# Feature interaction with attention: W's outputs and the pairs in halves, side by side on partitions

## What is computed

```python
e = jnp.stack([tbl_0[ids[:, 0]], ..., tbl_32[ids[:, 32]]], axis=1)       # 512 x 33 x 128
row, col = np.triu_indices(33, k=1)
inner = e[:, row] * e[:, col]                                            # 512 x 528 x 128
fm = relu(einsum('bpd,ad->bpa', inner, attn_W) + attn_b)
scores = einsum('ba,bpa->bp', gnn_feature, fm)
attn = softmax(scores, axis=1)
attn_output = einsum('bp,bpd->bd', attn, inner) * 100.0
h = concatenate([gnn_feature, attn_output, gnn_feature], axis=1)         # 512 x 384
y = relu(relu(h @ W_top1 + b_top1) @ W_top2 + b_top2) @ W_top3
```

## Time and profile before

| | |
|---|---|
| median of 3 runs | 659.28 us (658.95 to 659.39) |
| the profiled execution | 656.88 us, span 655.1 us |
| PE busy | 644.7 us, 98% |
| VectorE busy | 403.9 us, 62% |
| ScalarE busy | 434.0 us, 66% |
| GpSimd busy | 267.6 us, 41% |
| DMA | 17.28 MB, 24 GB/s to and from memory |

### The profile page before, as it was taken

One profiled execution on the slowest core, in us unless ns is written; L12 is line 12 of the kernel. 1 busy time (PEld: TensorE's weight loads), 2 busy tenths in 40 slices (PEclk: granted clock), 3 DMA queues, 4 the chain that ended last, 5 costly groups with the idle time before them and its releaser, 6 DMA issues.

```text
span 655.1 us, 22427 instructions
## 1 busy us (share of the span) xinstructions
PE 644.7 (98%) x9476; PEld 332.8 (51%) x9476; DVE 403.9 (62%) x426; ACT 434.0 (66%) x797; POOL 267.6 (41%) x208
## 2 busy tenths in 40 slices
PE   6999999999999999999999999999999999999998
PEld 2444444444444555444444555554444555545566
DVE  3555656565655667756565577765655567764763
ACT  2676677667777666766777666667677666677651
POOL 6888867585557223144746522234101011100010
PEclk9999999999999999999999999999999999999999
DMA  3311111120091111000092111000026011030020
GB/s 117 86 33 38 41 29 30 25 75 15 18 38 26 30 28 22 19 14 14 14 34 28 29 30 27 15 19 6 1 15 15 7 19 16 7 21 7 16 25 8
DMA packets 51285, 17.28 MB, mean 26 GB/s; under 512 B 47553, under 2 KB 48321, under 8 KB 51202
## 3 DMA queue, kind: packets, MB, share of 16 engines
q1 hardware_dynamic: 44738, 6.03, 11.2%
q0 software_dynamic: 4288, 8.66, 5.4%
q10 hardware_dynamic: 2176, 1.32, 0.7%
HBM read 14.10 MB, written 1.89 MB: 24 GB/s over the span
## 4 chain that ended last, share of the span: by engine, by line
PE 90%; POOL 4%; DMA 3%; issue 1%; DVE 1%; SPq 1%; ACT 0%; DVEq 0%
PE x_ps L465 65%; PE s_ps L477 16%; POOL rows L363 4%; PE m_ps L523 4%; PE m_ps L484 2%; DMA rows<-in_table,idx 1%; PE s_ps L563 1%; PE x_ps L563 1%; DMA band_scratch<-attn 1%; PE x_ps L523 1%; DMA idx_in<-in_ids 0%; DVE inner L749 0%; DMA tail_band<-band_scratch 0%; SPq L270 0%; PE m_ps L552 0%
## 5 line engine op out<-in xcount | busy, mean ns | idle before, releaser
L692 ACT ACTIVATE fm<-x_ps,ab 128x352 f32<-128x352 f32 x768 | 422.6, 554 | 188.4 <-PE x_ps L465 166.5
L465 PE MATMUL x_ps<-inner,attn_w_t 128*32 128x352 f32 x6144 | 478.7, 459 | 0.2 <-DVE inner L749 0.2
L465 PEld LDWEIGHTS x_ps<-inner,attn_w_t 128*32 128x32 f32 x6144 | 202.5, 110 | 225.6 <-issue 135.4
L749 DVE TENSOR_TENSOR inner<-e_t 128x2112 f32<-128x2112 f32 (+1 forms) x128 | 302.3, 2362 | 19.2 <-PE x_ps L465 16.7
L363 POOL DMA_INDIRECT rows<-in_table,idx x128 | 210.3, 1643 | 198.5 <-PE s_ps L477 183.1
L477 PE MATMUL s_ps<-fm,gnn_col 128*32 128x256 f32 (+1 forms) x2048 | 137.7, 386 | 0.0
L765 DVE COPY gnn_col<-gnn_z 128x8 f32<-128x8 f32 (+1 forms) x120 | 23.9, 199 | 183.9 <-PE s_ps L477 183.9
L477 PEld LDWEIGHTS s_ps<-fm,gnn_col 128*32 128x32 f32 x2048 | 68.5, 110 | 62.3 <-issue 19.0
L391 POOL TENSOR_TENSOR band<-band 128x192 f32<-128x192 f32 (+1 forms) x39 | 26.8, 687 | 145.1 <-DMA band<-band_scratch 144.6
L523 PE MATMUL m_ps<-band,rows 128*32 128x132 f32 x912 | 33.6, 275 | 0.0
L523 PEld LDWEIGHTS m_ps<-band,rows 128*32 128x32 f32 x912 | 28.0, 109 | 7.0
(11 more groups left out here) (53 smaller groups left out, 82.1 us busy)
## 6 DMA issues: line engine op xcount, KB each, us to landing
band<-band_scratch SPq DMA_DIRECT2D x144, 18.4 KB, 1.7
rows<-in_table,idx POOLq DMA_INDIRECT x128, 3.1
band_scratch<-zeros SPq DMA_DIRECT2D x1, 784.0 KB, 3.4
w<-in_W_top ACTq DMA_DIRECT2D x3, 256.0 KB, 3.6
band_scratch<-attn SPq DMA_DIRECT2D x12, 64.0 KB
gnn_z<-in_gnn_pairs SPq DMA_DIRECT2D x1, 512.0 KB, 6.0
w<-in_W_top ACTq DMA_DIRECT2D x1, 512.0 KB, 3.9
gnn_t<-in_gnn_cols SPq DMA_DIRECT2D x1, 256.0 KB, 3.9
```

The source lines that it names most:

```text
L465: mm = pe.matmul(strip(x_ps[:, (ROUNDS * slot + r) % 4, 0:ROUND], c), strip_of(attn_w_t, c), round_of(inner, slot, r), start=True, stop=True)
L692: act.activation(round_of(fm, slot, r), x_ps[:, (ROUNDS * slot + r) % 4, 0:ROUND], ACT.Relu, bias=ab[:, 0:1]).then_inc(fm_ready, 1)
L749: dve.tensor_tensor(inner[:, slot, :, :].rearrange("p q (i k) -> p q i k", k=HOPS), flat(e, at, [[P * WIDE, P], [WIDE, QUADS], [1, FIELDS] ...
```

## The change

The 128 outputs of W are cut in two halves of 64, and the 528 pairs of a sample in two halves of 264 (d from 1 to 8, and from 9 to 16). A round of PE is now one sample and one half of W: strips 0 and 1 work on the first half of the pairs, strips 2 and 3 on the second, so that a PSUM bank holds 64 outputs of 264 pairs on partitions 0 to 63 and the same outputs of the other 264 pairs on partitions 64 to 127. There are eight rounds of 264 columns a step.

The relus come out scaled: |g| relu(x + b) = relu(|g| x + |g| b), with `size` = |g| as scale and `shift` = |g| b as bias, both one value per partition. VectorE adds the two halves of W with their signs (`add_halves`, a scalar_tensor_tensor: second half times `turn_sign`, the product of the two signs, plus the first). The scores are then one matmul a sample over 264 columns with weights that are plus or minus one: two columns of a 32-column matrix, one for each half of the pairs. These weights lie in `diag`, which `set_diag` fills for four steps at once.

A sample's scores now take two rows of 264. A row group of 32 holds 16 steps, so a softmax stage is half a tile (`REGION`), in one of two PSUM banks; the last tile has stages of steps 0 to 15, 16 to 27 and 28 to 31. Maximum and sum are exchanged between neighbouring rows with `stream_shuffle`. The band is stored with 8 + 8 DMAs a stage. In the last tile five batches are pooled within the steps, from step 22 on, and 17 groups in the tail. The zeros of the band matrix are cleared by VectorE at the very start and stored then. `zeros`, `tail_band`, `h1` and `h2` share memory with `rows`. All loops over steps are unrolled. The core of the diff, with long stretches left out:

```diff
-            def pair_products(n, slot, first=False):
...
-                for r in range(ROUNDS):
...
-                        mm = pe.matmul(strip(x_ps[:, (ROUNDS * slot + r) % 4, 0:ROUND], c), strip_of(attn_w_t, c),
-                                       round_of(inner, slot, r), start=True, stop=True)
+            def pair_products(n):
+                slot = n % 2
+                pe.wait_ge(inner_ready, SIDES * n + SIDES)
+                for q in range(QUADS):
+                    for h in range(SIDES):
+                        bank = 2 * (q % 2) + h
...
+                            pe.wait_ge(rel_ready, ROUNDS * n + (2 * q + h - 3))
+                        for c in range(STRIPS):
+                            mm = pe.matmul(strip(x_ps[:, bank, 0:HALF], c), strip_of(attn_w_t, 2 * h + c % 2),
+                                           inner[:, slot, c // 2, q, :], start=True, stop=True)
...
-                for h in range(2):
-                    lo, hi = HALVES[h]
-                    for q in range(QUADS):
-                        mm = pe.matmul(s_ps[32 * q:32 * q + 32, h, score_at[h]:score_at[h] + hi - lo],
-                                       gnn_col[:, slot, q, :], fm[:, slot, q, lo:hi],
-                                       start=start, stop=stop, skip_group_check=reopened)
+                pe.wait_ge(fm_ready, QUADS * n + QUADS)
+                pe.wait_ge(diag_ready, n // 4 + 1)
+                for q in range(QUADS):
+                    mm = pe.matmul(s_ps[32 * q:32 * q + 32, r, 0:HALF], diag[:, m % REGION, q, :], fm[:, n % 2, q, :],
+                                   start=m % REGION == 0, stop=n + 1 in STAGE_END,
+                                   skip_group_check=t == LAST and m >= LATE_M)
...
-                    act.activation(round_of(fm, slot, r), x_ps[:, (ROUNDS * slot + r) % 4, 0:ROUND],
-                                   ACT.Relu, bias=ab[:, 0:1]).then_inc(fm_ready, 1)
+                        act.activation(rel[:, n % 2, q, h, :], x_ps[:, 2 * (q % 2) + h, 0:HALF], ACT.Relu,
+                                       bias=shift[:, h, b:b + 1], scale=size[:, h, b:b + 1]).then_inc(rel_ready, 1)
...
+                for h in range(SIDES):
+                    dve.tensor_tensor(
+                        inner[:, n % 2, h, :, :].rearrange("p q (i k) -> p q i k", k=HALF_HOPS),
...
+            def add_halves(n):
...
+                for q in range(QUADS):
+                    b = P * t + QUADS * m + q
+                    dve.wait_ge(rel_ready, ROUNDS * n + 2 * q + 2)
+                    dve.scalar_tensor_tensor(fm[:, n % 2, q, :], rel[:, n % 2, q, 1, :], turn_sign[:, b:b + 1],
+                                             rel[:, n % 2, q, 0, :], ALU.mult, ALU.add).then_inc(fm_ready, 1)
...
+            for n in range(2, STEPS * TILES):
...
+                product(n)
+                add_halves(n - 1)
+                if n % 4 == 2 and n + 2 < STEPS * TILES:
+                    set_diag(n // 4 + 1)
+                if n - 1 in STAGE_END:
+                    row_max(STAGE_END[n - 1])
+                if n - 2 in STAGE_END:
+                    normalise(STAGE_END[n - 2])
```

More of the change, by code:

```diff
@@ L71 @@
 LAST = TILES - 1
-L_POOL_AT = 25
-STAGE_M = (0, 18, 28, STEPS)
-L_BATCHES = STAGE_M[1] * QUADS // ROWS
+L_POOL_AT = 22
+REGION = STEPS // SIDES
+LATE_M = 28
+STAGES = tuple((t, r, REGION * r, REGION * r + REGION) for t in range(TILES) for r in range(SIDES))
+STAGES = STAGES[:-1] + ((LAST, 1, REGION, LATE_M), (LAST, 1, LATE_M, STEPS))
+STAGE_END = {STEPS * t + m1: k for k, (t, r, m0, m1) in enumerate(STAGES)}
+OPEN_STAGE, FINAL_STAGE = len(STAGES) - 2, len(STAGES) - 1
+L_BATCHES = REGION * QUADS // ROWS
 TAIL_ROW = ROWS * L_BATCHES
@@ L98 @@
 LAST_FIELDS_AT = 18
+WEIGH_AT = 14
 H1, H2 = 512, 256
@@ L264, in hidden, with attn_rows, issue_bands @@
             return h[:, :, at:at + end - start]
-        def issue_bands(queue, stage, m0, m1, main=range(QUADS), turned_around=range(QUADS), done=band_stored):
+        def attn_rows(q, h, r, m0, m1):
+            at = 32 * q + h - SIDES * REGION * r
+            return attn[at + SIDES * m0:at + SIDES * (m1 - 1) + 1:SIDES, r, :]
+        def issue_bands(queue, stage, main=range(QUADS), turned_around=range(QUADS), done=band_stored):
+            t, r, m0, m1 = STAGES[stage]
             queue.wait_ge(attn_ready, stage + 1)
@@ L644, in _ @@
+                if t == LAST and L_POOL_AT <= s < L_POOL_AT + L_BATCHES:
                     pool_step(LAST, s - L_POOL_AT)
-            scores(STEPS * TILES - 1, 1, stop=True, reopened=True)
+            scores(STEPS * TILES - 1)
             mlp_layer1(T2)
@@ L723, in _ @@
                           allow_slow_non_contiguous=True).then_inc(w23_loaded, 16)
-            for t in range(TILES):
-                base = STEPS * t
-                relus(base, 0, first=t == 0)
-                relus(base + 1, 1, first=t == 0, stage=t - 1 if t > 0 else None)
-                with act.Fori(1, 9 if t == LAST else 14) as i:
-                    for j in range(2):
-                        relus(2 * i + (base + j), j)
-                for s in range(18 if t == LAST else 28, STEPS):
-                    relus(base + s, s % 2,
-                          stage=LAST + STAGE_M.index(s - 1) - 1 if t == LAST and s - 1 in STAGE_M else None)
-            exp_rows(LAST + 2)
+            for n in range(STEPS * TILES):
+                relus(n)
+            exp_rows(FINAL_STAGE)
             for part in range(len(MLP_PARTS)):
@@ new lines, in take_signs @@
+            def take_signs(b0, b1, count):
+                dve.tensor_scalar(gnn_h[:, :, b0:b1], gnn_h[:, :, b0:b1], 0.0, 0.5, ALU.is_ge,
+                                  ALU.subtract).then_inc(half_signs_ready, 1)
+                dve.wait_ge(half_signs_ready, count)
+                dve.scalar_tensor_tensor(turn_sign[:, b0:b1], gnn_h[:, 0, b0:b1], 4.0, gnn_h[:, 1, b0:b1], ALU.mult,
+                                         ALU.mult).then_inc(turn_sign_ready, 1)
+                for h in range(SIDES):
+                    done = dve.tensor_scalar(signs[:, b0:b1, h], gnn_h[:, 0, b0:b1], side[:, h:h + 1], 2.0, ALU.mult,
+                                             ALU.mult)
+                done.then_inc(signs_ready, 1)
```

429 lines of the change are left out of this document (214 added, 215 removed).

## The result

The changed kernel takes 689.18 us (median of 4 runs, 686.76 to 691.90) beside 659.12 of the kernel before (658.88 to 659.39): ratio 1.046, 95% interval 1.042 to 1.050. The forecast was 649.0, its range ended at 670. The profiled execution took 687.09 at a span of 685.3. A run more than 1.5% above the fastest of its kernel counts as slow and stays out of the ratios: two of e6's four and one of e7's.

What follows compares the result with a forecast made beforehand. PE bound the kernel before, VectorE would after: last scores at 612.8 us plus a 32.0 tail gave a 644.8 span, 646.6 for the profiled execution, and 2.4 more for the median, 649.0 us; range 630 to 670.

Steps and rivals of the forecast that it cites:

- PE's step at 4.005: PE's time per plain step after the change: 3.56 us of pair products plus 0.445 of scores, saving 0.445.
- the 54 us off PE's path: PE's saving from step 7 to the last scores: 53.8 us over 121 steps, plus 0.7 for a pooling batch moved.
- the plain step at 3.99: VectorE's cost per step without pooling: half products 2.342 us, four adds 1.60, diagonal's copy 0.05; about equal to PE.
- Rivals 2 and 3: VectorE adds can't start early, 690 us, chance 0.12; ScalarE bound by two-pointer ACTIVATEs without overlap, 697 us, chance 0.05.
- 7.0 and 0.7 in the tail: Tail growth: first tail group 7.0 us later against the last scores, three more tail groups 0.7; summed there as 7.8.
- the 0.419 us: VectorE add's start-to-start time above which the median of before is reached, 0.019 over the forecast's value.
- The sum on VectorE: VectorE's work from step 7's adds to the last: 553.2 us, with 192.0 for 120 steps of adds.
- Its own waits vanish: VectorE, setting the pace from step 7 on, would hardly wait; 1.5 us added for steps where PE ends later.
- The argument for a packed queue: In each step, with PE's products done at T, ScalarE ends about T + 4.4, VectorE needs it at T + 5.1.
- Rival 4: The loop's ring of PE, ScalarE, adds, product stalls, or a last-tile band comes late: 5 to 20 us, chance 0.14.
- Opening +1.0: Opening up to step 7 lengthens by 1.0 us (bounds 0 and +3): step 7 at 52.7, its adds end at 57.5.
- The tail of 32.0: Time after the last scores: 22.8 us before, 30.6 with later first group and more groups, plus 1.4 for PE's clock.

Runs made afterwards that it cites:

- e6: The changed kernel with the adds and scores of a step done one step later: 679.15 us.
- e7: The changed kernel with every fourth step's halves added on PE and the other adds and scores one step later: 645.43 us, 0.980 of before.
- e1: The changed kernel without the adds, the scores reading only the first half of W's outputs: 631.11 us.
- e3: The changed kernel with GpSimd's folds of the band cut to one row group, the rest of the folding left out: 677.67 us.
- e2: The changed kernel with the constant 1.0 in place of the add's pointer to the sign: 679.43 us.
- e4: The changed kernel with every fourth step's halves added on PE by two score matmuls instead of VectorE's adds: 678.38 us, 2.8% slower than before.
- e5: The changed kernel with the zeros stored only after the scores of step 9, on the chip of e5 to e8: 670.79 us.
- e10: The changed kernel with the zeros stored only after the scores of step 9, run beside e9 on another chip than e5: 687.02 us.
- e8: The kernel of e7 with the zeros stored late and GpSimd issuing eight of the sixteen stores: 644.37 us, 0.977 of before; on a further chip 658.78, 1.001.
- e9: The changed kernel, unaltered, run again on the chip of e10: 691.27 us.

## Why the prediction was wrong

**Right**, with the measured value in brackets. PE's step at 4.005 (4.00 in e1), scores in two passes; of the 54 us off PE's path e1 got 46. VectorE as the new bound. The add at 485 ns (484), 0.40 apart (0.404), the pointer's 59 (58), the half product at 1256 (1250 alone), the plain step at 3.99 (3.95), the relu at 574 (579). Rivals 2 and 3 fell with these: instructions with a pointer do start early, so the rule of the Trainium skill (VectorE: DVE Perf Modes, "Two Vector instructions with no wait between them") agrees with the trace, and ScalarE is no bound. Two small slips change nothing: 7.0 and 0.7 in the tail are 7.7, not 7.8, and the 0.419 us at which the gain is gone is the value for 658 us; for 659.28 it is 0.421.

**Wrong**, against the forecast's own span of 644.8, 40.5 us:

1. *"The sum on VectorE", the adds at 1.600 a step.* This is the step that failed most: each add was priced alone. The 480 adds cost 19 us more than 192. Beside GpSimd's folds 29 last 735 and 17 last 762 ns for 484, together 12.0 more; e3 cut the folds short and got 11.9 back in the tiles that have them. The Trainium skill (SBUF — State Buffer, "Who interferes with whom") says that a VectorE instruction with two inputs from SBUF and a GpSimd instruction that reads SBUF contend for a shared port pair, that this is an exclusive lock, and that the order of issue decides who blocks. The trace agrees in the main. The pooling product, with one input from PSUM, lasts 546 ns on average alone and 556 to 562 beside a fold; three adds beside GpSimd's MEMSET, which only writes, last 481; 15 of the 18 products that were there first keep their length (1245 to 1259 ns), and the fold stretches. The adds show the order less clearly: the one that starts 0.54 us ahead of the fold's recorded start and the next are both some 0.27 us longer. The forecast should have weighed this rule and did not. The products cost 3.7 more, with some at 1.59 us for 1.25 beside a fold. Other small items came out 3 lower.
2. *"Its own waits vanish."* VectorE waited 11.7 us between step 7's adds and the last, not 1.5: 10.2 more. The argument for a packed queue gave the last relu at T + 4.4 and its use at T + 5.1, 0.7 of room; and where steps shrink (e2, e4) that room is gone. Rival 4 had this mechanism, and its 5 to 20 us hold the price; it lacked the longer adds. Part of these waits goes with the chip: 6.6 us in e5, 12.2 in e10, the same kernel.
3. *"Opening +1.0".* PE's step 7 started at 57.56 us, not 52.7, and its adds ended at 63.15, not 57.5: 5.7 late. Tile 0 stayed slow after it, part of point 2. Of tile 0's 11 us over the kernel before under 1 is the early zeros (e10); the rest goes with the chip and is open.
4. *The tail of 32.0* is 36.7. The mechanism was right, the 0.40 per store was not: 13.2 us for 16 stores, where 6.4 were reckoned. PE idled 10.9 us, not 7, and its clock fell.

These are 19 + 3.7 - 3 (VectorE's work), 10.2 (waits), 5.7 (opening) and 4.7 (tail), with rounding the 40.5 us.

On that clock: PE is at its lower level, 1.2 GHz, from 652.2 to 665.9 us of the span; it fell while PE idled for 10.9 us behind the last scores. The first tail group and the MLP group behind it lose 1.29 and 1.19 us, 2.5 together. The forecast took 1.4, half of the 2.8 for all of that work at the lower level. The Trainium skill (TensorE: Matmul & The Clock Gate, "Part 1: The HAM clock gate") has an idle PE return to the lower level, which leads to the 2.8; the trace is nearer to the page. In e7, where the same wait was longer, the MLP group is back at the full clock and only the first loses:

```profile
625.82 2.80 PE L582 MATMUL x_ps<-rows 128*32 128x132 f32 x48 [15.46 <-POOL rows L433]
628.55 2.05 PE L622 MATMUL s_ps<-rows,w 128*128 128x128 f32 x16
```

## What to carry over

Work moved to an engine with slack is priced with what runs beside it at that place, and GpSimd's rows show it too. Where two engines come out equal on paper, ask how much room the ring of waits between them has: less load gained 2.4 and 4.7 us a tile (e4), more room 1.3 and 1.1 (e6), both together 8.6 and 7.8 (e7). A gain near 2% that rests on such a ring is measured on more than one chip: e8's kernel is 2.3% faster on one and level on another. And before a difference between two kernels is put down to the edit, look whether the clock fell in one and not in the other: e9 and e10 differ in that too.

## What the runs showed of the hardware

- A two-input VectorE add of 264 columns lasts 484 ns alone, 735 to 762 on average beside GpSimd's fold, 630 beside its copy, 486 beside a gather, 481 beside its MEMSET.
- A store from every second partition takes 0.82 us to issue, of 12 KB or of 0.4 KB alike; the kernel before's, from neighbouring ones, 0.40 in the same place. No run changes the pattern alone.
- A pointer scalar costs a VectorE add of 264 columns 58 ns (484 against 426 in e2).
- The kernel before differs by 0.3% between chips, the changed one, with the zeros late, by 2.4% (670.8, a single run, and 687.0), 14 us of it in one tile.
- A fall of PE's clock to its lower level from 24.0 to 30.9 us, during a wait of 2.23 us, is there in e9 and not in the first profile of the same kernel; the first eight steps take 51.4 and 46.1 us.
